# Mamba layers of a four-stage kernel: the sum over states moves to TensorE, velocities in two passes

## What is computed

```python
delta = softplus(einsum('blr,er->ble', dbc[..., :16], dtw) + dtb)
dA = exp(delta[..., None] * -exp(a_log))
mi = delta[..., None] * Bm[:, :, None, :] * xb[..., None]
def scan_fn(carry, inp):                  # over the tokens
    h, v = carry
    dA_t, mi_t, C_t = inp
    v = 0.6 * v + mi_t                    # the velocity
    h = dA_t * h + v
    return (h, v), einsum('ben,bn->be', h, C_t)
y = (ys + dp * xb) * silu(z)              # then einsum('ble,de->bld', y, ow)
```

## Time and profile before

| | us |
|---|---|
| median of 3 runs (5295.73 to 5300.83) | 5296.98 |
| the profiled execution, its span | 5273.95, 5272.2 |
| busy: TensorE, VectorE, ScalarE, GpSimd | 3926.8, 3440.9, 2424.4, 1818.8 |
| first load of Mamba layer 0 to that of layer 1 | 1623.4 |
| from there to the load behind the layers | 1628.4 |

### The profile page before, as it was taken

How to read it: one execution, slowest core, us unless ns; L and a number is a source line. 1 busy time by engine, 2 the same in 40 slices (tenths; PEclk the granted TensorE clock), 3 DMA queues, 4 the chain that set the end, 5 groups by cost and what they waited for, 6 DMA issues and landing times. The chain is left out here.

```text
span 5272.2 us, 119189 instructions
## 1 busy us (share of the span) xinstructions
PE 3926.8 (74%) x41100; PEld 3133.2 (59%) x41101; DVE 3440.9 (65%) x6074; ACT 2424.4 (46%) x4814; POOL 1818.8 (34%) x1826
## 2 busy tenths in 40 slices
PE   6888799288888888888578778888788721788880
PEld 3555466276676676767456667677676621566660
DVE  3444422588888888888578888888888763333334
ACT  1111122266666566665465666656666520223320
POOL 1001000245445454454344544544545424000006
PEclk9888789587787787777677877777787755999995
DMA  1000000100000000000000000000000052100003
GB/s 42 0 0 0 18 0 0 46 2 2 2 2 2 2 2 2 2 2 2 15 2 2 2 2 2 2 2 2 2 2 2 1 215 76 41 30 30 30 27 96
DMA packets 50238, 93.91 MB, mean 18 GB/s; under 512 B 8946, under 2 KB 35442, under 8 KB 47028
## 3 DMA queue, kind: packets, MB, share of 16 engines
q1 hardware_dynamic: 40116, 60.89, 3.3%
q0 software_dynamic: 9600, 26.23, 1.5%
HBM read 51.42 MB, written 35.65 MB: 17 GB/s over the span
## 5 line engine op out<-in xcount | busy, mean ns | idle before, releaser
L922 DVE TENSOR_TENSOR_SCAN m_h<-m_dA,m_hlast,m_bank 128x256 f32<-128x256 f32 x2048 | 1358.9, 725 | 52.5 <-PE m_bank L1192 31.4
L1175 PE MATMUL m_bank<-ident,m_h 128*128 128x128 f32 x4096 | 739.2, 328 | 396.4 <-ACT m_prod L1048 191.1
L1192 PE MATMUL m_bank<-m_Mlo,m_Uhi 80*128 80x64 bf16 x8192 | 973.1, 210 | 61.0 <-issue 25.0
L1192 PE MATMUL m_bank<-m_Mhi,m_Ulo 80*128 80x64 bf16 x8192 | 969.0, 210 | 5.7 <-issue 5.7
L1192 PE MATMUL m_bank<-m_Mhi,m_Uhi 80*128 80x64 bf16 x8192 | 968.9, 210 | 0.0
L1192 PEld LDWEIGHTS m_bank<-m_Mlo,m_Uhi 80*128 80x128 bf16 x8192 | 844.8, 109 | 106.0 <-issue 45.0
L1038 ACT ACTIVATE m_dA<-m_delta,m_rate 128x256 f32<-128x256 f32 x2064 | 878.6, 501 | 32.8 <-issue 25.2
L1192 PEld LDWEIGHTS m_bank<-m_Mhi,m_Ulo 80*128 80x128 bf16 x8192 | 844.9, 110 | 45.4 <-issue 25.8
L1175 PEld LDWEIGHTS m_bank<-ident,m_h 128*128 128x128 f32 x4096 | 549.1, 167 | 497.4 <-issue 192.7
L1192 PEld LDWEIGHTS m_bank<-m_Mhi,m_Uhi 80*128 80x128 bf16 x8192 | 842.3, 109 | 0.0
L786 POOL TENSOR_TENSOR m_y<-m_y,m_prod 128x512 f32<-128x512 f32 x480 | 642.3, 1338 | 419.0 <-ACT m_prod L1048 419.0
(11 more groups left out here) (274 smaller groups left out, 7353.7 us busy)
## 6 DMA issues: line engine op xcount, KB each, us to landing
g_stage<-in_e_w SPq DMA_DIRECT2D x16, 1024.0 KB, 6.8
slots_x<-x_res SPq DMA_DIRECT2D x36, 256.0 KB, 7.4
x_x_in<-slots_x SPq DMA_DIRECT2D x72, 128.0 KB, 2.0
slots_y<-x_y POOLq DMA_DIRECT2D x72, 128.0 KB, 2.0
x_res<-in_x SPq DMA_DIRECT2D x1, 4096.0 KB, 13.9
parked<-x_res SPq DMA_DIRECT2D x1, 4096.0 KB, 13.5
so_residual<-parked SPq DMA_DIRECT2D x1, 4096.0 KB, 14.8
out_x<-x_res SPq DMA_DIRECT2D x1, 4096.0 KB, 13.6
```

The costliest lines, as they stand in the source:

```text
L922: nc.vector.tensor_tensor_scan(h[:, n % 3, m, :], dA[:, n % 3, m, :], VB[(n % 2) * 2 + m // 2][:, (m % 2) * CM:(m % 2 + 1) * CM], hlast[:, ...
L1175: last = nc.tensor.transpose(HB[tt][:, m * P:(m + 1) * P], h[:, n % 3, m, tt * P:(tt + 1) * P], net.ident[:])
L1192: last = nc.tensor.matmul(bank[:, at:at + SUB], u_part[:, par, jj, m * P:(m + 1) * P], m_part[:, par, jj, n, :], start=(i == 0), stop=(i = ...
```

## The change

**y.** GpSimd multiplies h by a row of C that stands in all partitions (`product`, hc = h * Cb, 128x1024 f32); TensorE adds the 16 products in two PSUM banks by matmuls with the identity (`accumulate`, two of 512 columns a slot, two slots behind). The rows of C go to memory once a chunk (`keep`) and come back to all partitions for two states at a time (`spread`). The transposes of h, prod, both sums of y and its transposes go; the last column is kept by ScalarE (`keep_last`).

**Velocity.** Two matmuls for three: high and low part of u over each other in 128 rows (U1 with M1), the rest with the carries in 112 rows (U2 with M2). M and u are made for two blocks at once in 128 partitions; SyncE's transfers lay them out (`place_m`, `place_u`, six each). All carries come from one sum of seven matmuls (`at == 17`) and nine transfers (`carries`), three more for the next chunk (`carry_next`).

**Order.** 16 slots a chunk; the head of chunk c + 1 starts five slots earlier (OFF), in the last slots of c - 1. Four buffers for h and dA (RING). The last chunk prepares none.

```diff
-KV = SUB + NS
+KV = SUB + 3 * NS
...
-LAG = 2
+RING, LEAD, OFF, NG = 4, 2, 5, 2
...
-        Bs, Cs = sb("Bs", [SUB, NSUB, NS]), sb("Cs", [P, 2, TM, NS])
...
-        dA = sb("dA", [P, 3, KI, CM])
-        h = sb("h", [P, 3, KI, CM])
+        Bs = sb("Bs", [P, TM, NS])
...
+        M1, M2 = sb("M1", [P, 2, NSUB, NS, SUB], BF16), sb("M2", [KV, 2, NSUB, NS, SUB], BF16)
+        Uhi, Ulo = sb("Uhi", [P, TM, DI], BF16), sb("Ulo", [P, TM, DI], BF16)
+        U1, U2 = sb("U1", [P, 2, NSUB, DI], BF16), sb("U2", [KV, 2, NSUB, DI], BF16)
+        Gf, Ghi, Glo = sb("Gf", [P, TM, NSUB, NS]), sb("Ghi", [P, TM, SUB], BF16), sb("Glo", [P, TM, SUB], BF16)
+        Gc = sb("Gc", [KV, SUB], BF16)
+        chi, clo = sb("chi", [SUB, DI], BF16), sb("clo", [SUB, DI], BF16)
+        dA = sb("dA", [P, RING, KI, CM])
+        h = sb("h", [P, RING, KI, CM])
...
-        y = sb("y", [P, 2, TM, DI])
-        prod = sb("prod", [P, 2, DI])
+        hc = sb("hc", [P, 2, KI, CM])
+        Cb = sb("Cb", [P, 2, NG, CM])
...
-        VB, HB, H0, H1 = banks[0:4], banks[4:6], banks[6], banks[7]
+        VB, Y, H0, H1 = banks[0:4], banks[4:6], banks[6], banks[7]
...
+                def spread(c, par, g):
+                    group = c * (NS // NG) + g
+                    sp.wait_ge(s["hc_done"], 1 + AHEAD + (group - 1) * NG)
+                    slot = g % 2
+                    rows = c_rows[par, g * NG:(g + 1) * NG].rearrange("n t -> (n t)")
+                    sp.dma_start(Cb[:, slot].rearrange("p n t -> p (n t)"), rows.partition_broadcast(P)
+                                 ).then_inc(s[f"c_spread{slot}"], 16)
+
+                def keep(q, par):
+                    sp.wait_ge(s["xp_done"], 1 + q + 1)
+                    sp.dma_start(c_rows[par], small[NS:2 * NS, :]).then_inc(s["c_kept"], 16)
+                    sp.wait_ge(s["c_kept"], 1 + 16 * (q + 1))
...
+                def place_m(q, par):
+                    sp.wait_ge(s["mlo_done"], 1 + q * TM + TM)
+                    for odd in range(2):
+                        rows = slice(odd * SUB, (odd + 1) * SUB)
+                        for to, of in ((M1[0:SUB], Mhi), (M1[SUB:P], Mhi), (M2[0:SUB], Mlo)):
+                            sp.dma_start(to[:, par, odd::2].rearrange("p j n t -> p j (n t)"),
+                                         of[rows].rearrange("p j n t -> p j (n t)")).then_inc(s["m_moved"], 16)
+
+                def place_u(q, par):
+                    sp.wait_ge(s["ulo_done"], 1 + q * TM + TM)
+                    for odd in range(2):
+                        rows = slice(odd * SUB, (odd + 1) * SUB)
+                        for to, of in ((U1[0:SUB], Uhi), (U1[SUB:P], Ulo), (U2[0:SUB], Uhi)):
+                            sp.dma_start(to[:, par, odd::2], of[rows]).then_inc(s["u_moved"], 16)
...
+                def move(par, row, j, sem):
+                    rows = slice(row * NS, (row + 1) * NS)
+                    for part, of in ((0, chi), (1, clo), (2, chi)):
+                        at = SUB + part * NS
+                        sp.dma_start(U2[at:at + NS, par, j, :], of[rows, :]).then_inc(sem, 16)
+
+                def carries(q, par):
+                    sp.wait_ge(s["clo_done"], 1 + q + 1)
+                    for j in range(1, NSUB):
+                        move(par, j - 1, j, s["moved"])
...
+                def slots(c, par, last, ending=False):
+                    for g in (1, 2, 3):
+                        spread(c, par, g)
+                    if not last:
+                        keep(c + 1, 1 - par)
+                    for g in (4, 5, 6):
+                        spread(c, par, g)
+                    if not last:
+                        place_m(c + 1, 1 - par)
+                        place_u(c + 1, 1 - par)
+                    spread(c, par, 7)
+                    if not last:
+                        carries(c + 1, 1 - par)
+                        spread(c + 1, 1 - par, 0)
+                        if not ending:
+                            carry_next(c, c + 1, par)
...
...
-                                nc.gpsimd.tensor_tensor(out, out, prod[:, n % 2, :], ALU.add).then_inc(s["y_pool"], 1)
+                def product(c, par, n):
+                    k = c * NS + n
+                    g = n // NG
+                    pool.wait_ge(s["scan_done"], 1 + AHEAD + (k + 1) * KI)
+                    pool.wait_ge(s["acc_done"], 1 + AHEAD + k - 1)
+                    if n % NG == 0:
+                        pool.wait_ge(s[f"c_spread{g % 2}"], 1 + 16 * (c * (NS // NG // 2) + g // 2 + 1))
+                    pool.sem_inc(net.carrier, 1)
+                    nc.gpsimd.tensor_tensor(hc[:, n % 2], h[:, n % RING],
+                                            Cb[:, g % 2, n % NG, :].unsqueeze(1).broadcast_to([P, KI, CM]), ALU.mult
+                                            ).then_inc(s["hc_done"], 1)
+
+                def slots(c, par, more, more2):
+                    for n in range(NS):
+                        if n >= 1:
+                            product(c, par, n - 1)
                         tail(c, 1 - par, n)
-                        head(c + 1, 1 - par, n)
+                        if more:
+                            head(c + 1, 1 - par, n + OFF)
+                        if more2 and n + OFF >= NS:
+                            head(c + 2, par, n + OFF - NS)
+                    product(c, par, NS - 1)
...
-                    if slot in (15, 16):
-                        for j in ((0, 1) if slot == 15 else (2, 3)):
-                            dve.wait_ge(s["uhi_done"], 1 + q * NSUB + j + 1)
-                            nc.vector.tensor_tensor(Ulo[0:SUB, par, j, :], (H0, H1)[j % 2][0:SUB, :],
-                                                    Uhi[0:SUB, par, j, :], ALU.subtract).then_inc(s["ulo_done"], 1)
-                    if slot == 16:
-                        for i in (0, 1, -1, 2, -2, 3, -3, -4):
...
+                    if at == 16:
+                        for j in range(TM):
+                            dve.wait_ge(s["uhi_done"], 1 + q * TM + j + 1)
+                            nc.vector.tensor_tensor(Ulo[:, j, :], (H0, H1)[j][:], Uhi[:, j, :], ALU.subtract
+                                                    ).then_inc(s["ulo_done"], 1)
+                    if at == 18:
+                        dve.wait_ge(s["chi_done"], 1 + q + 1)
+                        nc.vector.tensor_tensor(clo[:], H0[0:SUB, :], chi[:], ALU.subtract).then_inc(s["clo_done"], 1)
...
+                def scan(c, n):
+                    k = c * NS + n
+                    dve.wait_ge(s["hc_done"], 1 + AHEAD + k - RING + 1)
+                    dve.wait_ge(s["hlast_done"], 1 + AHEAD + k - RING + 1)
...
-                        if n >= LAG:
-                            k = c * NS + n - LAG
-                            out = y[:, par, 0, :]
-                            dve.wait_ge(s["ht_psum"], 1 + k * 2 + 2)
...
-                                nc.vector.scalar_tensor_tensor(out, HB[0][:], C, out, ALU.mult, ALU.add
-                                                               ).then_inc(s["y_dve"], 1)
+                    for n in range(NS):
+                        scan(c, n)
                         tail(c, 1 - par, n)
-                        head(c + 1, 1 - par, n)
+                        if more:
+                            head(c + 1, 1 - par, n + OFF)
+                        if more2 and n + OFF >= NS:
+                            head(c + 2, par, n + OFF - NS)
...
-                            nc.scalar.activation(prod[:, n % 2, :], HB[1][:], ACT.Copy,
-                                                 scale=Cs[:, par, 1, n - LAG:n - LAG + 1]).then_inc(s["prod_done"], 1)
...
+                def keep_last(c, n):
+                    act.wait_ge(s["scan_done"], 1 + AHEAD + (c * NS + n + 1) * KI)
+                    act.sem_inc(net.carrier, 1)
+                    nc.scalar.copy(hlast[:, n, :], h[:, n % RING, :, CM - 1]).then_inc(s["hlast_done"], 1)
...
+                    if at == 17:
+                        pe.wait_ge(s["moved_next"], 1 + 3 * 16 * q)
+                        pe.wait_ge(s["glo_done"], 1 + q + 1)
+                        pe.wait_ge(s["ulo_done"], 1 + q * TM + TM)
+                        pe.sem_inc(net.carrier, 1)
+                        nc.tensor.matmul(H0[0:SUB, :], Gc[SUB:KV, :], U2[SUB:KV, par, 0, :], start=True, stop=False)
+                        for j in range(TM):
+                            for part, of in ((Glo, Uhi), (Ghi, Ulo), (Ghi, Uhi)):
+                                last = nc.tensor.matmul(H0[0:SUB, :], part[:, j, :], of[:, j, :], start=False,
+                                                        stop=(j == TM - 1 and of is Uhi and part is Ghi))
+                        last.then_inc(s["carry_psum"], 1)
...
-                def turn(c, n):
+                def accumulate(c, n):
                     k = c * NS + n
-                    pe.wait_ge(s["scan_done"], 1 + (k + 1) * KI)
-                    for tt in (1, 0):
```

(52 more changed lines are left out.)

506 lines of the change are left out of this document (242 added, 264 removed).

## The result

The changed kernel takes 5017.6 us (median of 4 runs, 5011.1 to 5022.0) beside 5296.4 us for the kernel before: the ratio is 0.948, 95% interval 0.946 to 0.950. It is faster by 279 us, where the prediction said 520: its time lies in the range of 4560 to 5100, its sign is right, and the size is off by nearly a half.

The account below looks back on a forecast made before the run. VectorE was taken as nearest to a bound, with TensorE coming to the front. A chunk: net work 57.5 + exclusion 10 + TensorE's order 9 + clock 4 = 80 us for 94.5, giving 4777 us, range 4560 to 5100.

Parts of the forecast that it names:

- the part outside the chunks: Per layer outside the regular chunks: start 92 us, last chunk 57, end 17.
- the sum as two instructions: On TensorE, each f32 sum of 512 columns runs as two instructions: 1.7 us a slot at full clock.
- rival A: TensorE becomes the bound at today's clock: 77 us plus 9 to 15 of waits, 86 to 92 a chunk; 17%.
- Net work of VectorE: VectorE's work per chunk after the change, without exclusion: 57.5 us, of which 41 are scans.
- Exclusion: GpSimd's instructions and VectorE's with two SBUF inputs (or L837) exclude each other: 10 us a chunk, 3 to 19.
- The gate in slot 1: VectorE's gate needs TensorE's last sum, 9.1 us from the chunk's start against 5.1 of scans: a 4 us stall.
- The output product in slot 4: On TensorE, velocity, sum and output product stand behind scan 3, 6 us against 2.6 of scan 4: 2.5 us.
- The carries at the chunk's end: Nine transfers issued 0.4 us apart, then landing, before velocity 0 of the next chunk: 1 to 2 us of wait.
- The clock: TensorE's clock about 0.85, a third of the time half: 12 us a chunk, 4 counted on VectorE's path.
- Rival E: The transfers are late, so that velocity 0 or a product waits: 90 to 97 us a chunk; 5%.
- C: TensorE stays at the half clock through the layers: 118 us or more a chunk, 5917 or more, slower; 3%.
- D: GpSimd excludes VectorE's scans as well: 101 us a chunk, 5407 us, slower; 1%.

Follow-up runs that it names:

- half product: The changed kernel with GpSimd's product h*C for channel groups 0 and 1 alone, so half of y is left out: 4830 us, ratio 0.913.
- bfloat16: The changed kernel with the products h*C and the identity matrix of the sum in bfloat16 instead of float32: 4797 us, ratio 0.907.

## Why the prediction came out as it did

The frame was right in the main: VectorE and TensorE in turn through a chunk's first slots, the part outside the chunks, the net busy work, the sum as two instructions (1.9 us a slot for 1.7), scans that no product of GpSimd delays, and a sign with little doubt about it. Not in it was the chunk's second half, which hangs on GpSimd and then on SyncE's queue. The size was not: the forecast of 75 to 85 us a chunk, 4627 to 4927 us, missed. The range holds the time only because it was drawn to take in nearly all of rival A. A's mechanism, TensorE's whole busy time, is refuted by the sums 7 and 12 done twice, so that the range held is luck. The 8.8 us a chunk are these terms:

- **Net work of VectorE**, 57.5. Measured 70.3 less 13.0 of exclusion: 57.3. Right.
- **Exclusion**, 10 (3 to 19). Measured 13.0 in a chunk, each line less its length alone: the convolution 10.2 - 5.4 = 4.8 (the 13.4 of the half product's expectation counted its overlaps too), L961 2.75 - 1.15 = 1.6, L964 2.18 - 1.15 = 1.0, the pair L939 2.5 - 0.7 = 1.8, and 3.8 that the sum didn't have, the operations on 128x2, 4.1 for 0.3. I had priced the large operations, since the cost was thought of as a share of them; in these rows it is up to a whole instruction of GpSimd, whoever waits.
- **The gate in slot 1**, 4. Measured 5.8: TensorE reaches the last sum through half-clock stretches, and it starts them late, behind the late carries (see below).
- **The output product in slot 4**, 2.5 measured 5.8. This is the largest miss among TensorE's. The engine had stood idle for 3.4 us, so the velocity and the sum (3.76 us for 1.9) came one behind another at the lower clock, and the output product behind them. Two more sums there cost nearly all their length. The 2.5 was too low by its own figures as well: 6 us less the 2.6 of scan 4 is 3.4.
- **The carries at the chunk's end**, 1 to 2, measured about 5. The step that failed: "nine transfers ... issued 0.4 us apart". They are issued 0.63 us apart, and the queue is not free when they are due. I took the pitch from the loads of rows 2 (0.46 us apart on the mean) and added up the nine alone; the twelve of M and U ahead of them in the same queue stood in the count of bytes and nowhere in the count of issues. And they can't start before GpSimd has made M, of which the prediction said "It is not the bound": GpSimd's 25.4 us and the queue's 17.5 stand one behind the other. Six issues fewer at this place gave 124 us.
- **The clock**, 4 on VectorE's path for an assumed 0.85. In the chunks it was 0.90, in the span 0.856. The rate was no worse than assumed, but the half-clock stretches lie where TensorE has just waited (5.2 us before velocity 0, then 0.50 from 1411 to 1417; 3.4 us in slot 4, then 0.50 from 1353 to 1359), that is at the points that VectorE waits for. So the 4 us are inside the two terms above and in the smaller waits, not beside them.

In sum VectorE is busy for 70.3 us where 67.5 were expected, and idle for 18.5 where 13 were. Rival A has the right time (86 to 92 for 88.8) for a wrong reason: TensorE's whole busy time at the old clock. TensorE was busy 72 us, not 77, and work added in its free slots cost nothing. Rival E's time of 90 to 97 was near too, but the transfers themselves were not late (1.5 us from the last issue to the velocity); their issue was. C and D fell as argued.

What isn't settled: the half product's 187 us came almost all ahead of the end of M, but how much of them is GpSimd's own shorter work, how much exclusion in the convolution and in M, and how much of bfloat16's shortfall is the clock. An order in which M comes ahead of some products on GpSimd, or its transfers go in another order, wasn't tried, nor a kernel with the product on VectorE.
